# Late values and turned rows in the transposes' PSUM banks, ahead of the fourth projection and of the scores

## The reference

```python
# attention block: 8 heads of 32, windows of 64, each query sees its window and both neighbours
q, k, v = proj(Wq, bq), proj(Wk, bk), proj(Wv, bv)
scores  = where(band, q @ k3.T * 32**-0.5, -1e30)
o       = softmax(scores) @ v3
x1      = layernorm(xn + (o @ Wo + bo)) * gamma + beta
attn    = x1 + gelu(x1 @ W1 + b1) @ W2 + b2            # 256 -> 1024 -> 256
# sparse block: 8 experts, top 2 of a softmax gate
ffn     = sum_e w_e * (silu((xn @ gp_e) * (xn @ up_e)) @ down_e)   # 256 -> 816 -> 256
result  = x + attn + ffn
```

## Time and profile before

| what | us |
|---|---|
| median of 3 runs | 1146.22 (1145.24 to 1146.59) |
| the profiled execution | 1148.63 |
| its span in the trace | 1146.40 |
| PE busy | 1044.0 (91%) |
| DVE busy | 828.7 (72%) |
| ACT busy | 832.4 (73%) |
| POOL busy | 745.2 (65%) |

### The profile page before, as it was taken

One profiled execution on the slowest core, in us unless ns is written; L12 is line 12 of the kernel. 1 busy time (PEld: TensorE's weight loads), 2 busy tenths in 40 slices (PEclk: granted clock), 3 DMA queues, 4 the chain that ended last, 5 costly groups with the idle time before them and its releaser, 6 DMA issues.

```text
span 1146.4 us, 29415 instructions
## 1 busy us (share of the span) xinstructions
PE 1044.0 (91%) x8776; PEld 960.5 (84%) x8776; DVE 828.7 (72%) x1930; ACT 832.4 (73%) x1988; POOL 745.2 (65%) x1037
## 2 busy tenths in 40 slices
PE   2678999999999999989899999999999999999994
PEld 1456877777778777778899999999999999999994
DVE  3378466666666666654888888888888888888871
ACT  4565867676868686764788888887878887888782
POOL 5335646363636354532468888887888888888885
PEclk8789999999999999999899999999999999999997
DMA  9792012020201111401632222235721254125510
GB/s 313 228 307 64 25 61 69 28 66 30 64 32 54 42 37 37 159 34 57 210 92 34 37 37 37 37 66 151 217 61 31 37 149 97 30 37 152 163 48 2
DMA packets 62772, 98.36 MB, mean 86 GB/s; under 512 B 9424, under 2 KB 52432, under 8 KB 61072
## 3 DMA queue, kind: packets, MB, share of 16 engines
q1 hardware_dynamic: 47648, 78.16, 21.5%
q0 software_dynamic: 15088, 19.75, 9.1%
HBM read 130.13 MB, written 37.50 MB: 146 GB/s over the span
## 4 chain that ended last, share of the span: by engine, by line
PE 59%; ACT 12%; issue 8%; DVE 7%; DMA 6%; POOL 6%; POOLq 1%; ACTq 0%; DVEq 0%; SPq 0%
PE bank L1268 15%; PE bank L1269 15%; PE bank L1270 15%; DMA out_dram<-ys,dest 5%; POOL ht L634 4%; ACT sm L742 3%; DVE sm L1036 3%; PE bank L1361 3%; PE bank L1371 3%; PE bank L1399 3%; PE bank L1392 2%; DMA xg<-in_x_dram 2%; ACT pt L748 1%; POOL out_dram L646 1%; PE bank L1557 1%
## 5 line engine op out<-in xcount | busy, mean ns | idle before, releaser
L1268 PE MATMUL bank<-xt_h,gu_s 128*128 128x256 f32 (+1 forms) x1014 | 290.7, 287 | 6.5 <-DVE hf L1204 4.1
L634 POOL TENSOR_TENSOR ht<-hf,ht 128x256 fp32r<-128x256 f32 (+1 forms) x273 | 248.0, 917 | 61.9 <-ACT ht L847 51.4
L1269 PE MATMUL bank<-xt_l,gu_s 128*128 128x256 f32 (+1 forms) x1014 | 287.3, 283 | 0.0
L1270 PE MATMUL bank<-xt_h,gu_s 128*128 128x256 f32 (+1 forms) x1014 | 286.8, 283 | 0.0
L1191 DVE TENSOR_TENSOR gu_s<-raw_gu,gu_s 128x512 fp32r<-128x512 f32 (+1 forms) x273 | 201.0, 758 | 2.2 <-ACT gu_s L854 2.1
L1268 PEld LDWEIGHTS bank<-xt_h,gu_s 128*128 128x128 f32 (+1 forms) x1014 | 192.2, 190 | 8.4 <-issue 6.0
L1270 PEld LDWEIGHTS bank<-xt_h,gu_s 128*128 128x128 f32 (+1 forms) x1014 | 192.2, 190 | 0.0
L1269 PEld LDWEIGHTS bank<-xt_l,gu_s 128*128 128x128 f32 (+1 forms) x1014 | 191.6, 189 | 0.0
L836 ACT ACTIVATE gs<-bank,bias 128x256 f32<-128x256 f32 x234 | 110.0, 471 | 83.1 <-PE bank L1270 76.7
L646 POOL DMA_INDIRECT out_dram<-ys,dest x78 | 128.7, 1650 | 54.4 <-POOL ht L634 30.7
L742 ACT ACTIVATE sm<-sm,least 128x256 f32<-128x256 f32 x256 | 126.8, 499 | 23.1 <-DVE least L1036 23.0
(11 more groups left out here) (182 smaller groups left out, 2659.7 us busy)
## 6 DMA issues: line engine op xcount, KB each, us to landing
raw_gu<-in_gu_dram SPq DMA_DIRECT2D x39, 1648.0 KB
raw_dw<-in_dw_dram SPq DMA_DIRECT2D x39, 768.0 KB
xs_dram<-zrec SPq DMA_DIRECT2D x6, 1677.0 KB, 18.7
xr<-xs_dram SPq DMA_DIRECT2D x39, 258.0 KB
xwin<-xt_dram SPq DMA_DIRECT2D x8, 640.0 KB
raw_dw<-in_dw_dram SPq DMA_DIRECT2D x78, 64.0 KB
xg<-in_x_dram SPq DMA_DIRECT2D x8, 512.0 KB, 8.5
xt_dram<-xt SPq DMA_DIRECT2D x8, 512.0 KB, 3.6
```

Source lines behind the costliest of these rows:

```text
L634: nc.gpsimd.tensor_tensor(low, hf[0:m, ring(c), :], ht[0:m, p, 0, c, :].bitcast(F32), ALU.subtract).then_inc(h_split, 1)
L1268: nc.tensor.matmul(dst, lhs[0], rhs[0], start=start, stop=False)
L1269: nc.tensor.matmul(dst, lhs[0], rhs[1], start=False, stop=False)
L1270: return nc.tensor.matmul(dst, lhs[1], rhs[0], start=False, stop=stop)
```

## The change

The edits are all in the dense turn.

1. The values of the fourth and fifth tile (`V3`, `V4`) no longer take an `m_bank`. They go into `t_bank` 1 and 0, which are read out by then (`late_value`, `values_late`, `v_late`). Both now stand ahead of the fourth `out_project`.
2. The turned rows (`X0`, `X1`) go into `t_bank` 1 and 0 too (`turned_rows`), and both halves stand ahead of `scores(at, GT + 1)`. Before, the scores lay between them.
3. The list of `m_bank` uses is shorter by these four, so that `A3` and `O3` now have different banks, and `Y3` follows `O3` in its bank.
4. In slot 0, the first four chunks of `fill(1, ...)` are put ahead of `turn_probs` 2 and 3.
5. On ACT, `shares_copy` goes ahead of the last two pairs of exponentials in slots 0 to 2.
6. The counts of `t_full` and `t_free` get two more uses per turn (`t_count`).

```diff
-         "A2", "V2", "O3", "V3", "A3", "V4", "Y3", "X0", "X1"] + [f"F{c}" for c in range(FC1)])
+         "A2", "V2", "O3", "A3", "Y3"] + [f"F{c}" for c in range(FC1)])
...
+def t_count(bank, tile, uses, turn):
+    return tile * (3 - bank) + uses + 2 * turn.g
+
+def late_value(turn, j):
+    bank = GT - j
+    return bank, t_count(bank, turn.g * GT + GT, 1, turn)
+
+def turned_rows(turn, n):
+    return 1 - n, t_count(1 - n, turn.g * GT + GT, 1 if turn.seg == "last" else 2, turn)
...
@@ ACT, turn
                     if j == 0:
                         probs(at, 1, 1)
+                    shares_copy(at, j)
                     if j < GT - 1:
                         probs(at, j + 1, 2)
                         probs(at, j + 1, 3)
-                    shares_copy(g, j)
...
                         probs(at, GT, 0)
-                        v_copy(at, 3)
+                        v_late(at, 3)
                         probs(at, GT, 1)
...
-                    v_copy(at, 4)
+                    v_late(at, 4)
...
@@ DVE
             def x2_lo(at, n):
-                bk, free = full(f"X{n}", at)
+                b, uses = turned_rows(at, n)
+                dve.wait_ge(t_full[b], uses)
+                dve.wait_ge(m_hi, at.g * 2 + (n + 1))
...
@@ PE
+            def values_late(at, j):
+                b, n = late_value(at, j)
+                pe.wait_ge(t_free[b], n)
+                for k in range(KC):
+                    ins = passes(t_bank[b][:, 0:D], pair(xw_h, xw_l, every, k, slice(j * P, (j + 1) * P)), parts(wv_s, k, every), k == 0, k == KC - 1)
+                ins.then_inc(t_full[b], 1)
...
                 fill(0, *range(FC1))
+                fill(1, 0, 1, 2, 3)
                 half_slot(0)
-                fill(1, *range(FC1))
+                fill(1, 4, 5, 6, 7)
...
                 if more:
-                    values(at, 3)
+                    values_late(at, 3)
+                    values_late(at, 4)
                 out_project(at, 3)
-                if more:
-                    values(at, 4)
                 fill(3, *range(FC1))
                 turn_x2(at, 0)
+                turn_x2(at, 1)
                 if more:
                     scores(at, GT + 1)
-                turn_x2(at, 1)
```

More of the change, by code:

```diff
@@ L452, in _ @@
             turn(Turn("mid", NG - 2, NG - 3))
-            b, n = m_use("V4", Turn("mid", NG - 2, NG - 3))
-            sp.wait_ge(m_full[b], n + 1)
+            b, n = late_value(Turn("mid", NG - 2, NG - 3), GT)
+            sp.wait_ge(t_full[b], n)
             sp.wait_ge(slots_ready, 1)
@@ L729, in v_copy, with v_late @@
                 nc.scalar.activation(v[:, j, :, :], bk[:, 0:D].rearrange("p (h d) -> p h d", d=DH), ACT.Copy).then_inc(m_free[b], 1)
+            def v_late(at, j):
+                b, n = late_value(at, j)
+                act.wait_ge(t_full[b], n)
+                nc.scalar.activation(v[:, j, :, :], t_bank[b][:, 0:D].rearrange("p (h d) -> p h d", d=DH), ACT.Copy).then_inc(t_free[b], 1)
             def v_front(at):
@@ L743, in probs, with pt_copy, shares_copy @@
                                          accum_out=total[:, j % 2, c, r:r + 1]).then_inc(probs_ready, 1)
-            def pt_copy(g, j, r):
-                n = g * GT + j
-                act.wait_ge(t_full[r % 2], n * 3 + 2 if r == 2 else n * 2 + (r // 2 + 1))
+            def pt_copy(at, j, r):
+                act.wait_ge(t_full[r % 2], t_count(r % 2, at.g * GT + j, r // 2 + 1, at))
                 nc.scalar.activation(pt[:, r].rearrange("p a n -> p (a n)"), t_bank[r % 2][:, :], ACT.Copy).then_inc(t_free[r % 2], 1)
-            def shares_copy(g, j):
-                n = g * GT + j
-                act.wait_ge(t_full[0], n * 3 + 3)
+            def shares_copy(at, j):
+                act.wait_ge(t_full[0], t_count(0, at.g * GT + j, 3, at))
                 nc.scalar.activation(shares[:, j % 2, :], t_bank[0][:, 0:D], ACT.Copy).then_inc(t_free[0], 1)
@@ L756, in x2_hi @@
                 for n in range(2):
-                    bk = full(f"X{n}", at)
-                    nc.scalar.activation(x2t_h[:, :, n * BT:(n + 1) * BT], bk[:, :].rearrange("p (k c) -> p k c", k=KC), ACT.Copy).then_inc(m_hi, 1)
+                    b, uses = turned_rows(at, n)
+                    act.wait_ge(t_full[b], uses)
+                    nc.scalar.activation(x2t_h[:, :, n * BT:(n + 1) * BT], t_bank[b][:, :].rearrange("p (k c) -> p k c", k=KC), ACT.Copy).then_inc(m_hi, 1)
             def gelu(at):
@@ L782, in turn @@
                 for j in range(GT):
-                    pt_copy(g, j, 1)
+                    pt_copy(at, j, 1)
                     if j == 0:
@@ L790, in turn @@
                         v_copy(at, 2)
-                    pt_copy(g, j, 2)
+                    pt_copy(at, j, 2)
                     if more and j == 2:
@@ L1367, in turn_probs @@
                 pe.wait_ge(probs_ready, n * H + (2 * r + 2))
-                pe.wait_ge(t_free[r % 2], n * 2 + (r // 2 + 1) if r % 2 else n * 3 + (r // 2 + 1))
+                pe.wait_ge(t_free[r % 2], t_count(r % 2, n, r // 2 + 1, at))
                 for c in range(KC):
@@ L1386, in times_v @@
                 bk, full = take(f"O{j}", at)
-                pe.wait_ge(t_free[0], n * 3 + 3)
-                pe.wait_ge(t_free[1], n * 2 + 3)
+                pe.wait_ge(t_free[0], t_count(0, n, 3, at))
+                pe.wait_ge(t_free[1], t_count(1, n, 3, at))
                 for c in range(KC):
@@ L1402, in turn_x2 @@
             def turn_x2(at, n):
-                bk, full = take(f"X{n}", at)
+                b, uses = turned_rows(at, n)
+                pe.wait_ge(t_free[b], uses)
                 for j in range(2 * n, 2 * n + 2):
@@ L1414, in widen @@
                 for n in range(2):
-                    b, k = m_use(f"X{n}", at)
-                    pe.wait_ge(m_free[b], k + 1)
+                    b, uses = turned_rows(at, n)
+                    pe.wait_ge(t_free[b], uses + 1)
                     cs = slice(n * BT, (n + 1) * BT)
```

23 lines of the change are left out of this document (11 added, 12 removed).

## The result

| what | before | changed |
|---|---|---|
| median, measured side by side (4 runs each) | 1145.73 (1143.86 to 1146.59) | 1131.03 (1129.04 to 1133.75) |
| ratio | | 0.986, interval 0.984 to 0.988 |
| profiled execution, span | 1148.63, 1146.4 | 1132.38, 1130.3 |

The forecast was 1127.1 (range 1121.5 to 1136). The interval of the ratio is 13.6 to 18.3 us of gain. Where the 16.1 us between the two spans lie is read from the length of each slot, start to start of the weight loads of `turn_probs` group 0 that open it (slot 3 with the turn's end).

The account below looks back on a forecast made before the run. PE bounds the kernel, busy 54.8 of 58.55 us in a middle turn; only its holes can be won. Gains 9.0 + 7.1 + 1.0 + 0.7 + 1.3 = 19.1 us; 1146.22 - 19.1 = 1127.1, range 1121.5 to 1136.

Parts of the forecast that it names:

- The end of a middle turn: Turn's end: second half of widen starts 1.5 us earlier, 9.0 for six turns; bounds 0.5 and 1.7 per turn.
- Rival 1: Middle turn's end: the norm chain does not move, 0.5 instead of 1.5 per turn; gain 13.1, 1133.1 us; chance 0.10.
- Slot 0: Wait for exponentials goes: 0.9 in five turns, 1.3 in two, 7.1 us in all; bounds 0 and 1.3 per turn.
- rival 2: Slot 0: wide_share replaces the exponentials' wait, five turns gain nothing there; gain 14.6, 1131.6 us; chance 0.11.
- 0.15 a turn: Shares' copy ahead of exponentials: PE's next transposes wait less for bank 0; 1.0 us in seven turns, bounds 0 and 0.34.
- ACT comes near 195.4, behind shares turned by 195.0: Slot 0: ACT reaches the moved shares' copy only after the shares are turned, so moving it costs nothing.
- 5 x 0.9 + 2 x 1.3: Slot 0's sum, 7.1 us: 0.9 in five turns with POOL's subtraction there, 1.3 in the second and the last.
- the second and the last have not: Slot 0: these two turns lack POOL's subtraction there, so each gains the full 1.3 us.
- rival 4: Slower: POOL's late subtraction delays wide_share's copy and all behind it in five turns; 1149.6 us at 4.5 late; chance 0.04.
- POOL's slack of 14 us: POOL's waits for the residual's load: with this slack no queue can build up, said against the slower case.
- The first and the last turn: First turn's end 0.7 (bounds 0 and 1.5); last turn 1.3 (bounds 0.3 and 2): slot 2 0.7, end 0.6.
- The third stage: Not touched, keeps its 602.9 us; the prediction is wrong if its length changes.

Follow-up runs that it names:

- experiment 4: The changed kernel with the fifth tile's values (V4) behind the fourth projection again: 1135.91 us, ratio 0.9898.
- experiment 8: The changed kernel with the scores between the two halves of the turned rows again: 1130.34 us, ratio 0.9867.
- experiment 6: The changed kernel with POOL, from the third turn's round on, splitting the window before adding the residual: 1125.94 us, ratio 0.9825.
- experiment 2: The kernel before with only half of fill(1) put ahead of turn_probs 2 and 3: 1145.84 us, ratio 0.9983.
- Experiment 5: The changed kernel with POOL's first round reordered: two tiles' residual, bias, other two, window split only after slot 1's wide_share: 1126.29 us, ratio 0.9831.
- Experiment 1: The changed kernel with the fill(1) split and the earlier shares copy undone, only the turn's end new: 1137.38 us, ratio 0.9914.
- experiment 3: The kernel before with only the shares' copy put ahead of two pairs of exponentials: 1143.99 us, ratio 0.9984.
- experiment 11: The changed kernel with the shares' copy behind two pairs of exponentials again: 1137.46 us, ratio 0.9921.
- experiment 7: The changed kernel with POOL's order changed both in its first round and in its later rounds: 1124.06 us, ratio 0.9809.
- experiment 9: The changed kernel with both of POOL's reorderings and the scores between the two turned halves again: 1126.86 us, ratio 0.9833.
- experiment 10: The kernel before with half of fill(1) ahead of turn_probs 2 and 3 and the shares' copy earlier, old turn's end: 1137.16 us, ratio 0.9916.

## Why the prediction was right, and what of it was wrong

**The end of a middle turn: right.** The period was to fall to 56.1 and is 56.0. 1.5 was forecast for the second half of `widen`; it comes at 232.28 against 234.47 - 0.65, which is 1.54, and the whole slot is 1.64 shorter in each of six turns, 9.8 instead of 9.0. The path was right too: the square root 1.15 earlier (1.18 said), the norms 1.08 (0.98 said), the projection's wait at 0.31. Rival 1 fell. Experiments 4 and 8 split it: 1.08 for V4's place, 0.56 for the turned rows.

In experiment 4 the load ends at 230.70 and the square root starts at 230.71. The Trainium skill (ScalarE: Activation LUTs, "What ACT_TABLE_LOAD costs") gives 1.28 for the load and some 1.38 for a drain. With that drain, the end could not have gained 1.64; no run here shows one ahead of the square root.

**Slot 0: the size right, the cause half wrong.** 0.9 forecast, 0.80 measured over five turns (4.0 instead of 4.5), and 1.32 and 1.22 for 1.3 in the second and the last. What the copy of `wide_share` keeps back is 0.5 by experiment 6, where 0.35 was said; rival 2, that it keeps all, fell, though its time (1131.6) is the nearest to the measured one: its number would have been right by luck. But the prediction put the gain down to edit 4 and called edit 5 0.15 a turn. It said of ACT's copy that "ACT comes near 195.4, behind shares turned by 195.0", which is where the copy comes *with* edit 5. It never asked where the copy would come without: behind two more pairs of exponentials, 10.9 after the slot's opening in experiment 2, where 195.4 is 9.1 after it. The trace of the kernel before already had that copy at 196.86. That slot 0 came near its forecast all the same rests on both edits being in the change. Slot 0 by edits:

| slot 0, regular turn | without edit 5 | with edit 5 |
|---|---|---|
| without edit 4 | 11.59 | 11.59 |
| with edit 4, old end | 11.34 | 10.21 |
| with edit 4, new end | 11.32 | 10.79 |

**The second turn: the step that failed.** The sum has "5 x 0.9 + 2 x 1.3" in slot 0 and 1.5 at the end for this turn too, since "the second and the last have not" the subtraction there. The second has it one slot further on. In the regular turns POOL's chain hangs on the residual's load and so on PE's own last turn, and it follows PE at a distance. In the second turn it hangs on the scatter behind the gate: POOL's first residual add started at 130.15 before and 130.76 now, while PE came 2.2 earlier. So PE ran into it: 4.15 lost in slots 1 and 2, of which the 1.18 of slot 2 stand at the lower clock behind the waits. Experiment 5 gives 4.2 back by moving POOL alone. This is the mechanism of rival 4 (the copy under the subtraction, with all behind it late) in one turn instead of five; the prediction had excluded it by POOL's slack of 14 us, which the first round does not have. The row it cited says so: 7 waits for the residual's load in eight rounds; the first round's wait is the one for the scatter's DMA, 1.89.

**The first and the last turn: right, though the pair before and changed shows it badly.** They gave 1.0 for 0.7, and 2.0 for 1.3 + 1.3 + 0.15, with the last turn's own end giving nothing. In the first turn the whole 1.0 lies in slots 1 and 2, at a higher granted clock than before (0.84 and 1.00 for 0.79 and 0.91), and the end shows nothing, at a lower one (0.88 for 0.94). Experiment 1 has the clock of the kernel before in all four slots, and its end is 0.64 shorter, near the forecast's 0.7. The last turn's slot 2 gave 0.93 (0.7 forecast), as experiments 3 and 11 confirm; in experiments 6 to 9, at a lower clock in that slot (0.80 to 0.91 instead of 0.96), it took 8.05 to 8.19. Its end took 36.13 at 0.96 where the kernel before had 35.84 at 0.98; experiment 3, with the old end and 0.96 too, took 36.69, so the new end gives 0.56, the forecast's 0.6.

**The third stage** was said to keep its 602.9, or the prediction was wrong. It was 601.4, and between 598.0 and 601.0 in the experiments, which leave it alone. The single 602.9, at a mean clock of 0.98 where the changed kernel had 0.99, was the longest of all profiled executions, and the criterion was too strict: some 1.5 of the 16.1 us of span are not the change's.

Together: 19.1 forecast, + 0.8 (ends), - 0.6 (slot 0), - 0.1 (edit 5's slots), + 0.3 (first turn), - 0.7 (last turn's slot 2 and end, 0.6 for 1.3), - 4.15 (second turn, slots 1 and 2) is 14.7 by the turns. That the medians give the same to a tenth says little: their interval is 13.6 to 18.3, and the terms of the first and the last turn hold the clock of one execution each.

## What to carry to other kernels

When PE is made faster, ask of each other engine's round what it hangs on: work that follows PE stays at its distance, work that hangs on a DMA chain or on the first stage does not, and PE runs into it, first of all in the first rounds. Two edits that each close one of two waits in a row have no separate prices: follow the queue behind the first wait to the next release, and try them together. If an engine has to switch tables before the op that everybody waits for, move its last op of the old kind ahead.

## What the runs showed of the hardware

- A copy of 0.29 us on DVE takes 2.68 when it starts behind POOL's subtraction, and ended 0.15 to 0.16 after it in the first three cases shown (142.96, 143.56, 194.76). Not all of DVE stands still: under the same subtraction, from 140.14 to 142.81, DVE's add `x<-bank,xb` took its usual 0.42. Subtractions of two SBUF operands are held like the copy (experiment 7: 3.59 for two, against 0.85 for the one that started ahead of the subtraction). The Trainium skill (SBUF — State Buffer, "Who interferes with whom") says so of copies and of two SBUF inputs, and that one SBUF input does not contend; these rows agree.
- The lower clock came behind PE's stalls. After its waits of 1.12 and 1.75 in the second turn the granted clock was 0.51 from 147.4 to 150.9 (the 1.2 GHz level), though PE was busy throughout it; the slot behind, at a mean of 0.91, took 1.2 us more for the same work. Among the 13 profiled kernels, the six whose slot 1 took 11.5 us or more in the second turn (the changed one and experiments 2, 4, 6, 8 and 10) show such a stretch there, and the seven that took 10.0 or less do not.
- The same slot at another granted clock: slot 0 of the first turn took 7.86 at 1.00 (2.4 GHz) and 9.76 at 0.65, the end 25.86 at 1.00 in experiment 4 and 27.70 at 0.88 in the changed kernel. Before a difference of two single profiles is put down to an edit, the clock of the two windows has to be compared.
